# A causal mask in attention, added by VectorE in PSUM instead of by a product on TensorE

## What is computed

```python
scores = jnp.einsum('bkgqd,bkpd->bkgqp', qg, k) * scale
causal = jnp.tril(jnp.ones((s, s), dtype=bool))
scores = jnp.where(causal, scores, jnp.float32(-1e+30))
probs = jax.nn.softmax(scores, axis=-1)
out = jnp.einsum('bkgqp,bkpd->bkgqd', probs, v).reshape(b, H, s, D)
```

## Time and profile before

| | value |
|---|---|
| median of 3 runs | 4,822.86 us |
| profiled execution | 4,827.4 us, span 4,825.6 us |
| mean granted clock | 0.956 |
| PE busy | 4,247.8 us, 88% |
| DVE busy | 3,382.5 us, 70% |
| ACT busy | 2,776.1 us, 58% |
| POOL busy | 2,195.7 us, 46% |
| row maxima (L1741) | 1,301 operations, 778.0 us busy |
| `low` (L1761) | 1,280 operations, 780.0 us busy |
| exponentials (L1693) | 812.9 us busy |

### The profile page before, as it was taken

One profiled execution on the slowest core, in us unless ns is written; L12 is line 12 of the kernel. 1 busy time (PEld: TensorE's weight loads), 2 busy tenths in 40 slices (PEclk: granted clock), 3 DMA queues, 4 the chain that ended last, 5 costly groups with the idle time before them and its releaser, 6 DMA issues. The chain is left out here.

```text
span 4825.6 us, 80545 instructions
## 1 busy us (share of the span) xinstructions
PE 4247.8 (88%) x19000; PEld 2919.8 (61%) x19031; DVE 3382.5 (70%) x7206; ACT 2776.1 (58%) x6565; POOL 2195.7 (46%) x1795
## 2 busy tenths in 40 slices
PE   7888888789999979999999999999954549999996
PEld 3333333346666557777777777777743437777775
DVE  6999999944433868888888888888844443333336
ACT  7777777522221038888888888888822214444441
POOL 5989999710000024435343544444445643333330
PEclk8999999999999989999999999999976769999999
DMA  1000000021101551212122121212154425455548
GB/s 44 14 14 14 14 27 9 9 85 61 45 17 38 180 145 37 63 46 63 37 65 63 44 63 39 70 37 63 37 177 144 146 98 159 153 153 154 157 139 349
DMA packets 291467, 394.38 MB, mean 82 GB/s; under 512 B 67744, under 2 KB 213920, under 8 KB 285744
## 3 DMA queue, kind: packets, MB, share of 16 engines
q1 hardware_dynamic: 218288, 274.39, 19.0%
q0 software_dynamic: 26112, 73.44, 4.3%
q10 hardware_dynamic: 46944, 45.16, 3.5%
HBM read 239.81 MB, written 153.03 MB: 81 GB/s over the span
## 5 line engine op out<-in xcount | busy, mean ns | idle before, releaser
L1761 DVE TENSOR_TENSOR probsT<-ps_t,probsT 128x512 fp32r<-128x512 f32 (+3 forms) x1280 | 780.0, 609 | 118.7 <-ACT probsT L1701 102.8
L1693 ACT ACTIVATE probs<-ps_s,negm 128x512 f32<-128x512 f32 (+3 forms) x1297 | 812.9, 627 | 35.1 <-DVE negm L1754 34.2
L1541 PE MATMUL ps_o<-probsT,vbuf 128*128 128x512 f32 (+3 forms) x2560 | 824.0, 403 | 5.9
L1516 PE MATMUL ps_s<-kbuf,qbuf 128*128 (+1 forms) x2602 | 771.9, 381 | 58.2 <-ACT probs L1693 31.5
L1741 DVE TENSOR_REDUCE pmax<-ps_s 128x1 f32<-128x512 f32 (+3 forms) x1301 | 778.0, 601 | 50.7 <-PE ps_s L1516 27.2
L1701 ACT ACTIVATE probsT<-ps_t 128x512 fp32r<-128x512 f32 (+3 forms) x1280 | 686.1, 536 | 170.9 <-PE ps_t L1529 146.1
L1529 PE MATMUL ps_t<-idn,probs 128*128 128x128 f32 x4352 | 695.3, 275 | 16.8 <-DVE probsT L1761 16.8
L527 POOL TENSOR_TENSOR dBx<-u,b_all 128x1024 f32<-128x1024 f32 x255 | 611.9, 2410 | 96.1 <-DVE h L623 66.1
L1529 PEld LDWEIGHTS ps_t<-idn,probs 128*128 128x128 f32 x4352 | 517.8, 141 | 158.3 <-DVE probsT L1761 28.1
L1516 PEld LDWEIGHTS ps_s<-kbuf,qbuf 128*128 128x128 f32 x2602 | 445.6, 189 | 197.1 <-ACT probs L1693 69.3
L285 PE MATMUL ps_y<-hc,idn 128*128 128x512 f32 x1024 | 495.7, 606 | 34.0 <-POOL hc L535 32.4
(11 more groups left out here) (272 smaller groups left out, 6996.4 us busy)
## 6 DMA issues: line engine op xcount, KB each, us to landing
room_b<-xs ACTq DMA_DIRECT2D x294, 136.0 KB
room_a<-q_scr SPq DMA_DIRECT2D x528, 64.0 KB
room_c<-y SPq DMA_DIRECT2D x32, 1024.0 KB, 8.5
room_a<-W_guT SPq DMA_DIRECT2D x64, 384.0 KB
q_scr<-rot SPq DMA_DIRECT2D x64, 256.0 KB, 2.9
rspread<-r_scr SPq DMA_DIRECT2D x64, 256.0 KB
attn_T<-ostage SPq DMA_DIRECT2D x128, 128.0 KB, 2.3
at<-attn_T SPq DMA_DIRECT2D x32, 512.0 KB
```

The costliest lines, as they stand in the source:

```text
L1516: last = nc.tensor.matmul(ps_s[:, u % RING, 0:w], qbuf[:, BAND * s + j, :], kbuf[:, bass.ds(kslot, 1), part, c * CW:c * CW + w], start=par ...
L1541: last = nc.tensor.matmul(ps_o[:, lo:], vbuf[:, kb, :, :], probsT[:, g % SLOTS, part, lo:], start=kb == 0 and part == 0, stop=kb == BAND * ...
L1693: nc.scalar.activation(probs[:, k, at:at + n, :], ps_s[:, u % RING, 0:n * P], ACT.Exp, bias=negm[:, tile, :], accum_out=sums[:, s, j, c:c ...
L1761: nc.vector.tensor_tensor(probsT[:, g % SLOTS, 1, lo:], ps_t[:, t % 2, lo:], probsT[:, g % SLOTS, 0, lo:].bitcast(F32), ALU.subtract).then ...
```

## The change

The mask product and what it needs (`idn_r`, `mask_r`, the two roundings on ACT, `rounded`) are taken out. In its place DVE adds the mask tile to the last 128 columns of a diagonal chunk, in place in PSUM, ahead of the chunk's row maximum, and the maximum waits for that addition by a new semaphore, `masked`. DVE and PE wait for the constants at their start.

```diff
@@ constants and semaphores
-        idn_r = sb("idn_r", [P, P], F32R)
-        mask_r = sb("mask_r", [P, P], F32R)
-        rounded = tally("rounded")
+        masked = tally("masked3", QT)
@@ scores, on PE
-                                            start=part == 0, stop=part == 1 and c < s)
-                if c == s:
-                    last = nc.tensor.matmul(ps_s[:, u % RING, w - P:w], idn_r[:, :], mask_r[:, :], start=False, stop=True)
+                                            start=part == 0, stop=part == 1)
                 last.then_inc(s_done.sem, 1)
-            pe.wait_ge(rounded.sem, 2)
+            pe.wait_ge(consts.sem, 16 * NCONST)
@@ ahead of the loops, on ACT
-            act.wait_ge(consts.sem, 16 * NCONST)
-            for dst, src in ((idn_r, idn), (mask_r, mask)):
-                nc.scalar.activation(dst[:, :], src[:, :], ACT.Copy).then_inc(rounded.sem, 1)
@@ peak, on DVE
+                w = blocks(s, j, c) * P
                 dve.wait_ge(s_done.sem, s_done.at(hx, u + 1))
-                nc.vector.reduce_max(pmax[:, tile, c:c + 1], ps_s[:, u % RING, 0:blocks(s, j, c) * P],
+                if c == s:
+                    nc.vector.tensor_tensor(ps_s[:, u % RING, w - P:w], ps_s[:, u % RING, w - P:w], mask[:, :],
+                                            ALU.add).then_inc(masked.sem, 1)
+                    dve.wait_ge(masked.sem, masked.at(hx, 2 * BAND * k + tile + 1))
+                nc.vector.reduce_max(pmax[:, tile, c:c + 1], ps_s[:, u % RING, 0:w],
                                      axis=mybir.AxisListType.X).then_inc(cmax.sem, 1)
@@ ahead of the loops, on DVE
+            dve.wait_ge(consts.sem, 16 * NCONST)
             dve.wait_ge(high_k.sem, high_k.at(0))
```

## The result

The change made the kernel slower: 4,882.1 us against 4,823.8 for the kernel before beside it, a ratio of 1.0123, with an interval of 1.0108 to 1.0137. The forecast was 4,889 us, 1.4% slower. The profiled execution has a span of 4,880.8 us against 4,825.6.

A forecast was written before the change was run, and what follows sets the result against it. PE (97% busy) and DVE, as full as PE in two stretches of a head, were taken to bound it. Lateness of 0.8 + 1.2 = 2.0 us per head gave 64, plus 2 for the prologue: 4,889 us, range 4,845 to 4,950.

The forecast's parts named there:

- Price of a mask, 0.32 us: On DVE per mask: addition 0.29 plus the maximum's wait 0.03, with bounds of 0.21 and 0.42 us.
- Why the gap is 0.03: Between addition and maximum on DVE: 0.03 rather than 0.13 us, as the maximum has only one new wait in front.
- The first rival, the free wait: Maximum's wait on DVE costs nothing, 0.21 us per mask, 0.9 per head, 4,853 us; chance 0.15.
- Unit 0, 1.1 late at step 15: Unit 0, steps 0 to 15: six masks, 1.95 us against 0.85 taken in; DVE 1.1 late, PE 0.3 to 0.4.
- Unit 0's end, 0.8 late: End of unit 0: DVE's waits for ACT absorb part of the 1.1; 0.8 us late coming out at the next unit.
- Unit 1, 0.46 by step 7, 0.74 by step 11 and 1.2 at the end: Unit 1: masks in chains over `negm` pass their delay, steps 16 and 17 add nothing; 1.2 us late at the end.
- PE's 1.2 us is swallowed: Removed products on PE, 1.2 us per head: where PE waits for DVE or ACT, finishing sooner only lengthens its wait.
- The head, 55.6 to 55.7, x 32 = 64 us: One head of `attention`: 0.8 + 1.2 = 2.0 us longer, 64 us over 32 heads.
- The start: DVE's first operation waits for the constants, holding PE's start by `k_ready`; all of attention starts some 0.3 us later.
- The prologue, 2 us: Eight masks in a chain with no `low` between: at most 8 x 0.32, taken as 2 us.
- PE setting the pace: Whole head: DVE keeps up, masks lengthen no chain, head falls by PE's 1.2 us, 38 us, 4,785; chance 0.07.
- All passes: Whole head: the absorbing slack is itself another wait; head grows 3.9 to 5.5 us, 4,950 to 5,000; chance 0.10.

The follow-up runs named there:

- e2: Kernel after with the mask product put back on PE and its two roundings on ACT, so the mask is added twice; 4,891.0 us.
- e1: Kernel before, product kept, plus the same DVE addition written to an unused SBUF tile, so the maximum doesn't wait for it; 4,848.6 us.
- e4: Kernel before with only band 3's four masks per head moved to DVE, the others left on PE; 4,865.2 us.
- e6: Kernel before with only band 0's four masks per head (steps 16 to 19 of unit 1) moved to DVE; 4,825.9 us.
- e10: Kernel after with each mask added behind the maximum and `negm`; ACT waits for the addition only at the diagonal chunk; 4,814.6 us.
- e12: Kernel after with only band 3's masks added behind the maximum and `negm`, the others ahead of the maximum; 4,852.5 us.
- e8: Kernel after with `low` put between addition and maximum in the steps that have a `low`; 4,969.1 us.
- e11: Kernel after with addition and maximum fused for bands 0 to 2, and band 3's masks added behind the maximum and `negm`; 4,808.5 us.
- e3: Kernel before without the mask product, DVE unchanged, so the causal mask is left out altogether; 4,797.3 us.
- e7: Kernel after with addition and row maximum of a diagonal chunk in one DVE operation, over the chunk's whole width; 4,820.7 us.

## Why the prediction was right

- *Price of a mask, 0.32 us.* Right in both terms: 289 ns for the addition, 0.034 us between its end and the maximum. A result in PSUM costs what one in SBUF does (289 against 281 to 289 ns). The bound of 0.42 didn't occur.
- *Why the gap is 0.03.* The number held, its reason doesn't follow from the rows. Rows 7 and 8 were told apart by what `negm` has to wait for. In the code every `negm` waits by two semaphores, and in the kernel before the gap ahead of it is 0.126 at 128, 256 and 384 columns, and at band 3's 512 as well:

```profile
2356.79 0.68 DVE L1741 TENSOR_REDUCE pmax<-ps_s 128x1 f32<-128x512 f32 x1
2357.60 0.16 DVE L1754 TENSOR_REDUCE negm<-pmax 128x1 f32<-128x4 f32 x1
```

  Of the tiles in the loop whose `negm` follows its maximum directly only band 2's last has 0.034, and why it has, no run shows. That the maximum, which waits for the addition by one semaphore, would have the short gap was a choice between two values that came out well.
- *The wait counts.* Right, and it was more than the third of the price that it looks like: e2 less e1 is 1.34 of a head's 1.81. The first rival, the free wait, is e1: forecast 4,853, measured 4,849, with the product still on PE. So had the wait been free, the time would have been about that, or a little less. The Trainium skill (VectorE: DVE Perf Modes, The DRAIN you can't avoid) has it that a semaphore between two operations of DVE adds nothing; here the measurement decides against it: the rows of e1 and after, 0.08 before the end against 0.034 behind it, show 0.12 us per mask.
- *Unit 0, 1.1 late at step 15.* That stretch is 1.18 us longer, and the `low` of step 15 starts 1.22 later within its head. Six masks of 0.32 are 1.94, so 0.72 was taken in where I had 0.85: the overlap regained was a little less than I gave it. The transposes of step 17 start 0.41 later within the head, where I had 0.3 to 0.4. PE waits for `low` earlier than I said, though, from step 7 on.
- *Unit 0's end, 0.8 late.* Measured 0.6. The term was too large: the two waits of `low` for ACT vanished whole, so that the `low` of step 18, which had the second, was only 0.5 late. PE's wait at the place of 2332.57 grew from 0.35 to 0.50, as the chain wants.
- *Unit 1, 0.46 by step 7, 0.74 by step 11 and 1.2 at the end.* Measured 0.52 in steps 0 to 7, a further 0.69 in steps 8 to 19, so 1.21 in all. Right to 0.06. e4 shows that these are band 3's four masks (1.19) and e6 that steps 16 to 19 add nothing, as the step said. (The working's own additions give 0.72 and 1.04 at steps 11 and 15, where it has 0.74 and 1.06.)
- *PE's 1.2 us is swallowed.* Right in kind: e2 against after gives back 0.23. It isn't nothing, as the step had it, but it is a fifth.
- *The head, 55.6 to 55.7, x 32 = 64 us.* Measured 55.48, 1.81 x 32 = 58. The miss of 6 us is 0.2 per head. By stretches it is unit 0's end; but it is also what the removed product gave back (0.23), a term that the working had at next to nothing. With the product kept, e2 lies 2.03 above the kernel before, where I had 2.0; it is made of 0.65 in unit 0 and 1.38 in unit 1, where I had 0.8 and 1.2. So the two halves missed in opposite directions, and that the sum is this close is in part luck.
- *The start.* PE's first product was to be held by DVE's first operation, and is:

```profile
1744.00 2.74 DVE L1775 TENSOR_TENSOR kbuf<-room_a,kbuf 128x2048 fp32r<-128x2048 f32 x1 [18.43 <-DMA mask<-causal]
...
1746.79 3.91 PE L1514 MATMUL ps_s<-kbuf,qbuf 128*128 128x512 f32 x10 [22.14 <-DVE kbuf L1775]
...
1770.95 0.69 DVE L1759 TENSOR_TENSOR probsT<-ps_t,probsT 128x512 fp32r<-128x512 f32 x1 [0.60 <-ACT probsT L1697]
```

- *The prologue, 2 us.* Too large. From PE's first product to the first `low` it is 24.16 us, against 23.53 in the trace of before: +0.6 (e2 has 1.3 by the same measure, and e10 and e12, also with all masks on DVE, 0.1 less than before; these are single traces). DVE waits for `scores` ahead of most maxima there, and the additions fell into that. The absolute start, 1746.79 in place of 1750.65, isn't the change's doing: e8, e10 and e12, which have the same start as the kernel after, begin at 1750.51 to 1751.99, and e1 and e2, which make DVE wait for the same constants, at 1750.92 and 1751.36. So the sum of this trace is 58 + 0.6 - 3.9 = 55, and the span grew by 55.2.
- *What the profile would show.* DVE's busy time grew by 3.5 us per head, to 50.6 (91%), not by 4.6 to 52: busy time counts an overlap once, and each addition overlaps its predecessor by 0.08. That was a slip of reading, without effect on the sum. PE's share is 93% as said. PE waits for `low` and for the exponentials 6.6 us per head by its loads, 3.0 and 3.6, where more than 5 was said.
- *The rivals of the other side.* PE setting the pace needed masks below 0.14 us; e11 reaches it in effect (53.01), by overlap and by leaving the chain, not by a cheaper addition. "All passes" fell: of 5.1 us of new DVE time per head 2.0 came through, and 1.8 with the product's gain. The rule of the Trainium skill (Perfetto Trace Analysis, Identifying the Most-Contended Engine) by which DVE is the contended engine gave the right sign, but e3 shows that PE was no bystander: without its product the kernel before gains 0.67 per head.

## What to carry to other kernels

Before work is moved to an engine with free time, ask where in the loop that free time lies and whether the new operation stands on a chain that another engine waits for: here the same 0.32 us cost 0.30 at four places, 0.07 at eight and nothing at four. Put such an operation behind the result that others wait for, if the arithmetic lets you (here the maximum may cover what is masked later), and avoid a wait of an engine for its own last operation, which costs its overlap. And when an operation is moved in front of another, count not only its duration but what it waits for itself (e8).

## What the runs showed of the hardware

- Two DVE operations that follow each other without a dependence overlap by 0.08 us; with a wait of the second for the first by one semaphore there is a gap of 0.034 (e1 and the kernel after, 520 pairs each). The difference, 0.12 us, is the price of each such wait, on top of the operation. Where `negm`, which waits by two semaphores, directly follows its maximum in the loop, the gap is 0.126 for every tile but one.
- An addition of 128x128 in fp32 with its result in place in PSUM takes 289 ns in the kernel after, and 281 ns with its result in SBUF in e1.
- The fused addition and maximum takes as long as the maximum alone, 0.69 us at 512 columns and 0.29 at 128, but brings a second instruction of 141 ns, of which 0.06 to 0.07 us is seen at the end (e7).
- PE's product of 128 columns, 0.06 us from start to start and 0.11 on a narrow chunk, was worth 0.67 us per 16 in the kernel before, and 0.23 in the kernel after, where PE waits for DVE.
